# First attention: the query's norm factor moves into the exponential's scale, and epsilon into a column of the sum of squares

## What is computed

```python
q = jnp.einsum('btd,ndh->btnh', x, q_kernel)       # 16 heads of 128
kv = jnp.einsum('bsd,ckdh->cbskh', x, kv_kernel)   # 8 key/value heads
q = rms_norm(q, q_norm_scale)                      # x * rsqrt(mean(x^2) + 1e-6) * scale
k = rms_norm(k, k_norm_scale)
q = apply_rope(q, positions); k = apply_rope(k, positions)
mask = (j <= i) & (i - j < 128)
logits = jnp.einsum('btkgh,bskh->bkgts', qg * ATTN_SCALE, k)   # 2 query heads to a key head
probs = jax.nn.softmax(jnp.where(mask, logits, min), axis=-1)
enc = jnp.einsum('bkgts,bskh->btkgh', probs, v)
return jnp.einsum('btnh,nhd->btd', enc, out_kernel)
```

## Time and profile before

| | before |
|---|---|
| median of 3 runs | 1593.5 us |
| profiled execution | 1587.25 us, span of its instructions 1585.4 us |
| PE busy | 1478.0 us (93%) |
| DVE busy | 1085.6 us (68%) |
| ACT busy | 882.6 us (56%) |
| POOL busy | 403.2 us (25%) |
| first attention | 0 to about 658 us of the span |

### The profile page before, as it was taken

One profiled execution on the slowest core, in us unless ns is written; L12 is line 12 of the kernel. 1 busy time (PEld: TensorE's weight loads), 2 busy tenths in 40 slices (PEclk: granted clock), 3 DMA queues, 4 the chain that ended last, 5 costly groups with the idle time before them and its releaser, 6 DMA issues.

```text
span 1585.4 us, 24036 instructions
## 1 busy us (share of the span) xinstructions
PE 1478.0 (93%) x7582; PEld 1095.0 (69%) x7582; DVE 1085.6 (68%) x2404; ACT 882.6 (56%) x2052; POOL 403.2 (25%) x473
## 2 busy tenths in 40 slices
PE   4899999999998999799999999999879999999898
PEld 3788788878887888667777777777644444444476
DVE  6898699859976998377555455455438676767654
ACT  4777677757785777444332332332236565756556
POOL 4666566566655665200000000000000000000000
PEclk9999999999999999899999999999969899999999
DMA  6000000000000000233000000000030000000001
GB/s 236 1 1 1 1 1 1 1 3 1 1 1 3 1 1 1 66 91 90 20 1 1 0 0 0 0 0 0 2 135 1 1 1 0 0 0 0 1 14 40
DMA packets 15767, 28.54 MB, mean 18 GB/s; under 512 B 2000, under 2 KB 10064, under 8 KB 15024
## 3 DMA queue, kind: packets, MB, share of 16 engines
q1 hardware_dynamic: 15264, 26.51, 4.9%
q0 software_dynamic: 400, 0.78, 0.3%
HBM read 25.96 MB, written 2.10 MB: 18 GB/s over the span
## 4 chain that ended last, share of the span: by engine, by line
PE 73%; DVE 10%; issue 6%; POOL 5%; ACT 4%; DMA 1%; DVEq 0%; SPq 0%; ACTq 0%; POOLq 0%
PE ps L1126 13%; PE ps L1128 13%; PE ps L1127 13%; PE ps L1396 5%; PE ps L1179 5%; PE ps L1455 4%; PE ps L1225 4%; PE ps L1240 2%; PE ps L1377 2%; POOL rope L388 2%; PE ps L1523 2%; PE ps L1206 2%; DVE ssum L528 1%; PE ps L1281 1%; PE ps L1409 1%
## 5 line engine op out<-in xcount | busy, mean ns | idle before, releaser
L360 POOL TENSOR_TENSOR ln_rs<-ln_ve,minus_half 128x4 f32<-128x4 f32 x16 | 17.4, 1085 | 887.5 <-DVE ln_ve L424 887.5
L710 DVE TENSOR_REDUCE nm<-ps 128x1 f32<-128x512 f32 x256 | 168.3, 687 | 70.2 <-PE ps L1396 68.4
L1126 PE MATMUL ps<-xnT_lo,w1moe_hi 128*128 128x512 f32 x400 | 177.4, 444 | 2.4 <-DVE w2moe_lo L665 2.2
L1044 ACT ACTIVATE pT<-ps 128x512 f32<-128x512 f32 x256 | 143.5, 601 | 62.6 <-PE ps L1409 60.2
L960 ACT ACTIVATE moe_act_hi<-sg 128x512 fp32r<-128x512 f32 x100 | 63.3, 633 | 190.6 <-DVE sg L642 190.6
L1127 PE MATMUL ps<-xnT_hi,w1moe_lo 128*128 128x512 f32 x400 | 160.5, 401 | 0.0
L1128 PE MATMUL ps<-xnT_hi,w1moe_hi 128*128 128x512 f32 x400 | 159.9, 400 | 0.0
L388 POOL TENSOR_TENSOR rope<-rope 128x384 f32<-128x384 f32 x128 | 144.2, 1127 | 0.0
L632 DVE TENSOR_TENSOR sg<-ps,sg 128x512 f32<-128x512 f32 x100 | 69.1, 691 | 96.0 <-ACT sg L980 96.0
L892 ACT ACTIVATE raw<-ps 128x512 f32<-128x512 f32 x128 | 76.4, 597 | 99.3 <-PE ps L1128 97.0
L912 ACT ACTIVATE prob<-ps,nmax 128x256 f32<-128x256 f32 (+1 forms) x256 | 113.2, 457 | 30.8 <-DVE nmax L503 30.7
(11 more groups left out here) (204 smaller groups left out, 3747.3 us busy)
## 6 DMA issues: line engine op xcount, KB each, us to landing
yT<-in_w1moe SPq DMA_DIRECT2D x25, 256.0 KB, 2.6
encT<-in_wqkv SPq DMA_DIRECT2D x8, 512.0 KB, 8.7
w_in<-in_w2moe SPq DMA_DIRECT2D x25, 128.0 KB, 2.7
wo<-in_wo SPq DMA_DIRECT2D x1, 2048.0 KB, 19.1
wm<-in_wm SPq DMA_DIRECT2D x2, 1024.0 KB, 11.9
out_x<-x_res SPq DMA_DIRECT2D x4, 512.0 KB, 2.9
x_res<-in_x SPq DMA_DIRECT2D x1, 1536.0 KB, 14.7
pT<-in_c_pick SPq DMA_DIRECT2D x1, 1024.0 KB, 5.6
```

What stands on the lines that cost most here:

```text
L710: V.tensor_reduce(nm1[:, m % 2, t, col:col + 1], ps[:, 2 + i % 2, :], AX.X, ALU.max, negate=True).then_inc(s1_max, 1)
L1044: A(pT1[:, u % 2, 2 * (m % 2) + h, c, :], ps[:, 4 + e % 2, :], ACT.Exp, scale=SCALE1).then_inc(p1_ready, 1)
L1126: MM(out, left[0], right[1], start=first, stop=False)
```

## The change

1. The query heads are no longer multiplied by their factor. VectorE multiplies only the key (`kn`, 128 columns for 384), and TensorE turns the queries straight from `rope1`.
2. The query's factor is the scale operand of the exponential, one number in each row. The row maximum is then of unscaled scores, so a new VectorE instruction multiplies it by the factor: `nshift` is `nmax` times `rms`, two numbers in a row, and is the exponential's bias.
3. Epsilon is a 129th column in the buffer of the squares, set once, and is summed with them. GpSimd's addition `msq` is gone.
4. `rms` is kept in six buffers, not two, since the exponential reads it four steps later. The waits follow: GpSimd's power waits for the exponential of six steps back, ssum for the turn of the tile two before it.

```diff
-                    nc.gpsimd.tensor_tensor(msq[:, s, :], ssum[:, s, :], eps_sum[:], ALU.add).then_inc(meaned, 1)
-                    pool.wait_ge(meaned, k + 1)
-                    nc.gpsimd.tensor_tensor(rms[:, s, :], msq[:, s, :], minus_half[:, 0:3],
+                    if n >= RMS_RING:
+                        pool.wait_ge(prob_ready, k - RMS_RING + 1)
+                        pool.wait_ge(qk_normed, k - RMS_RING + 1)
+                    nc.gpsimd.tensor_tensor(rms[:, n % RMS_RING, :], ssum[:, s, :], minus_half[:, 0:3],
                                             ALU.pow).then_inc(rms_ready, 1)
                     pool.wait_ge(roped, k + 1)
-                    nc.gpsimd.tensor_tensor(rope1[:, s, :], rope1[:, s, :], rope2[:, s, :],
+                    nc.gpsimd.tensor_tensor(rope1[:, s, :].rearrange("p (h f) -> p h f", h=3),
+                                            rope1[:, s, :].rearrange("p (h f) -> p h f", h=3), rope2[:, s, :, 0:P],
                                             ALU.add).then_inc(rotated, 1)
...
                     dve.wait_ge(scored, k + 1)
+                    if m >= 2:
+                        dve.wait_ge(prob_ready, k - 1)
                     V.tensor_reduce(nmax[:, s, :], ps[:, 3 + s, :].rearrange("p (h f) -> p h f", h=2)[:, :, 0:w],
-                                    AX.X, ALU.max, negate=True).then_inc(max_ready, 1)
+                                    AX.X, ALU.max, negate=True).then_inc(maxed, 1)
+                    dve.wait_ge(maxed, k + 1)
+                    V.tensor_tensor(nshift[:, s, :], nmax[:, s, :], rms[:, m % RMS_RING, 0:2], ALU.mult
+                                    ).then_inc(max_ready, 1)
...
-                    V.tensor_tensor(qkn[:, s, :].rearrange("p (h f) -> p h f", h=3),
-                                    rope1[:, s, :].rearrange("p (h f) -> p h f", h=3),
-                                    rms[:, s, :].unsqueeze(2).to_broadcast((P, 3, P)), ALU.mult
+                    V.tensor_scalar(kn[:, s, :], rope1[:, s, 2 * P:3 * P], rms[:, m % RMS_RING, 2:3], None, ALU.mult
                                     ).then_inc(qk_normed, 1)
...
                     if n >= 2:
-                        dve.wait_ge(rotated, k - 1)
-                        dve.wait_ge(qk_normed, k - 1)
-                    V.reduce_sum(ssum[:, s, :], sq[:, s, :].rearrange("p (h f) -> p h f", h=3), AX.X
-                                 ).then_inc(summed, 1)
+                        dve.wait_ge(rms_ready, k - 1)
+                        dve.wait_ge(qk_turned, k - 1)
+                    V.reduce_sum(ssum[:, s, :], sq[:, s, :, :], AX.X).then_inc(summed, 1)
...
                         ins = A(prob[:, m % PROB_RING, h, 0:w], ps[:, 3 + s, h * 2 * P:h * 2 * P + w], ACT.Exp,
-                                bias=nmax[:, s, h:h + 1], accum_out=psums[:, s, h:h + 1])
+                                bias=nshift[:, s, h:h + 1], scale=rms[:, m % RMS_RING, h:h + 1], accum_out=psums[:, s, h:h + 1])
...
-                        ins = T(ps[:, 5 if m < EARLY_TURNS else 2, h * P:(h + 1) * P], qkn[:, m % 2, h * P:(h + 1) * P], ident[:])
+                        turned = rope1[:, m % 2, h * P:(h + 1) * P] if h < 2 else kn[:, m % 2, :]
+                        ins = T(ps[:, 5 if m < EARLY_TURNS else 2, h * P:(h + 1) * P], turned, ident[:])
```

More of the change, by code:

```diff
@@ L33 @@
 STEPS = GROUPS * TT
-RAW_RING, QK_RING, PROB_RING = 9, 4, 3
+RAW_RING, QK_RING, PROB_RING, RMS_RING = 9, 4, 3, 6
+SQ = P + 1
 LAST_LAG = 8
@@ L93, in build @@
         minus_half = sb("minus_half", [P, 16])
-        eps_sum = sb("eps_sum", [P, 3])
         spare = sb("spare", [P, 2])
@@ L107, in build @@
         ssum = sb("ssum", [P, 2, 3], where=part_a)
-        msq = sb("msq", [P, 2, 3], where=part_a)
-        rms = sb("rms", [P, 2, 3], where=part_a)
+        rms = sb("rms", [P, RMS_RING, 3], where=part_a)
         qkT = sb("qkT", [P, QK_RING, 3, P], where=part_a)
         nmax = sb("nmax", [P, 2, 2], where=part_a)
+        nshift = sb("nshift", [P, 2, 2], where=part_a)
         psums = sb("psums", [P, 2, 2], where=part_a)
@@ L117, in build @@
         rope1 = sb("rope1", [P, 2, 3 * P], where=part_a)
-        rope2 = sb("rope2", [P, 2, 3 * P], where=part_a)
-        qkn = sb("qkn", [P, 2, 3 * P], where=part_a)
+        rope2 = sb("rope2", [P, 2, 3, SQ], where=part_a)
+        kn = sb("kn", [P, 2, P], where=part_a)
         odd_head = [sb(f"odd_head_{part}", [P, SEQ], F32R, part_a) for part in ("hi", "lo")]
@@ L224, in build @@
         projected, raw_kept, squared = sem("projected"), sem("raw_kept"), sem("squared")
-        summed, meaned, rms_ready = sem("summed"), sem("meaned"), sem("rms_ready")
+        summed, rms_ready = sem("summed"), sem("rms_ready")
         roped, rotated, qk_normed = sem("roped"), sem("rotated"), sem("qk_normed")
@@ L228, in build @@
         scored, max_ready, prob_ready = sem("scored"), sem("max_ready"), sem("prob_ready")
+        maxed = sem("maxed")
         inv_ready, probn_ready = sem("inv_ready"), sem("probn_ready")
@@ L350, in _ @@
             nc.gpsimd.memset(minus_half[:], -0.5).then_inc(half_set, 1)
-            nc.gpsimd.memset(eps_sum[:], HD0 * RMS_EPS).then_inc(half_set, 1)
+            nc.gpsimd.memset(rope2[:, :, :, P:SQ], HD0 * RMS_EPS).then_inc(half_set, 1)
             pool.dma_start(ident_b[:], dram["c_ident"]).then_inc(masks_loaded, 16)
@@ L380, in attention_step @@
                     pool.wait_ge(summed, k + 1)
-                    if n >= 2:
-                        pool.wait_ge(qk_normed, k - 1)
-                    nc.gpsimd.tensor_tensor(msq[:, s, :], ssum[:, s, :], eps_sum[:], ALU.add).then_inc(meaned, 1)
-                    pool.wait_ge(meaned, k + 1)
-                    nc.gpsimd.tensor_tensor(rms[:, s, :], msq[:, s, :], minus_half[:, 0:3],
+                    if n >= RMS_RING:
+                        pool.wait_ge(prob_ready, k - RMS_RING + 1)
+                        pool.wait_ge(qk_normed, k - RMS_RING + 1)
+                    nc.gpsimd.tensor_tensor(rms[:, n % RMS_RING, :], ssum[:, s, :], minus_half[:, 0:3],
                                             ALU.pow).then_inc(rms_ready, 1)
                     pool.wait_ge(roped, k + 1)
-                    nc.gpsimd.tensor_tensor(rope1[:, s, :], rope1[:, s, :], rope2[:, s, :],
+                    nc.gpsimd.tensor_tensor(rope1[:, s, :].rearrange("p (h f) -> p h f", h=3),
+                                            rope1[:, s, :].rearrange("p (h f) -> p h f", h=3), rope2[:, s, :, 0:P],
                                             ALU.add).then_inc(rotated, 1)
@@ L533, in attention_step @@
                     rh = r3.rearrange("p (h f) -> p h f", h=3)
-                    o2 = rope2[:, s, :].rearrange("p (h f) -> p h f", h=3)
+                    o2 = rope2[:, s, :, 0:P]
                     V.tensor_tensor(o2[:, :, 0:H2], rh[:, :, H2:HD0], sin3[:, t, :, 0:H2], ALU.mult)
@@ L894, in attention_step @@
                         act.wait_ge(rotated, k - 1)
-                    A(sq[:, s, :], ps[:, s, 0:3 * P], ACT.Square).then_inc(squared, 1)
+                    A(sq[:, s, :, 0:P], ps[:, s, 0:3 * P].rearrange("p (h f) -> p h f", h=3), ACT.Square).then_inc(squared, 1)
                 if new and 2 <= n < STEPS + 2:
```

## The result

The changed kernel takes 1615.6 us (median of 4 runs, 1615.14 to 1616.13), the kernel before 1592.85 us beside it (4 runs, 1591.81 to 1593.52): ratio 1.015, interval 1.013 to 1.0171, so 23 us slower. The profiled execution took 1615.93 us with a span of 1614.1 us; the mean granted clock was 0.973, before 0.976.

The account below looks back on a forecast made before the run. TensorE was taken to set the pace at 3.83 us a step, with a VectorE-GpSimd loop close behind. Terms 14.4 + 4.4 - 6.0 + 4.0 = +16.8 us gave 1604 from the profiled execution, 1610 from the median; range 1586 to 1621.

Parts of the forecast that it names:

- item 4: Mid-batch loop, steps 8 to 31: VectorE becomes the pace, 15.90 against 15.30 us per four steps, costing 14.4 us.
- item 8: Batch ends: exponentials' second column and late nmax with nshift are uncovered, 1.0 us a batch, 4.0 in all, bounds 0 and 6.
- Item 1: GpSimd without msq: the add starts 1.77 us after ssum, not 2.12, gaining 0.35, held back by the sine products.
- Item 2: Add meets the prob multiplies: pair ends at 3.16 (add between, likelier) or 3.21 (add first), making prob and nmax 0.74 us later.
- Item 3: VectorE's rest of a step: nshift adds 0.2 us (bounds nothing to 0.56), kn replaces qkn for 0.3 less.
- item 5: Next batch's layer norm on VectorE: half of 2.2 us no longer hidden, 4.4 us over four batches, bounds 0 and 8.8.
- Item 6: First steps of a batch, before any prob: earlier add and shorter kn gain 1.5 us a batch, -6.0, bounds 0 and -9.0.
- item 7: Exponential's scale column: up to 0.10 us each, 0.2 a step, hidden by ScalarE's wait for TensorE; 25 us if uncovered.
- A: Second prob multiply keeps its turn or the add isn't ready; loop 3.6 us, TensorE still the pace: -5.4, 1588 us; chance 0.25.
- C: The exponentials' second column becomes the bound, not the collision: 25 us uncovered, 1612 us; chance 0.04.
- D: Multiple signal waits of kn, nshift and ssum add 0.1 us a step to the pace, 10 us: 1620 us; chance 0.10.
- B: Collision makes VectorE slip only in some steps, or half its price is made up: 1593 to 1596 us; chance 0.09.

Follow-up runs that it names:

- e2: The kernel before with only the epsilon column (msq removed), queries still multiplied, no nshift or second column: 1620.8 us, ratio 1.0156.
- e6: The changed kernel without nshift, the exponential's bias being the plain maximum: 1589.93 us, ratio to before 0.9993.
- e1: The changed kernel with epsilon added on GpSimd again (msq before the power): 1588.28 us, ratio to before 0.9973.
- e5: The changed kernel with the exponential's scale a constant again, the query's norm factor left out: 1609.82 us, ratio to before 1.0117.
- e4: The changed kernel with one more wait: GpSimd's add starts only after the prob multiplies of VectorE's next step: 1590.99 us.
- e11: The changed kernel with msq back on GpSimd and without nshift, the bias being the plain maximum: 1580.83 us, ratio to before 0.9947.

## Why the prediction was right

The mechanism was the one forecast and the time came in at 1615.6 for 1610, but items 4 and 8 were too small, and the difference between a median and a profiled execution hid part of that.

- Item 1, the start of the add. It was to come 1.77 after ssum's start and came 298.10 - 296.25 = 1.85. I had the power at 0.91, as in the earlier trace rows, from where msq had started. Alone it takes 1.23, so taking msq out advances the add by 0.27, not 0.35, and it is the power, not the sine products, that it waits for. It is still early enough to meet the multiplies, and e2 shows that on the kernel before this alone makes the loss.
- Item 2, the collision. The pair was to end 3.16 or 3.21 us after ssum's start, by which goes first, and ends 299.42 - 296.25 = 3.17. Of the two orders that I gave, it is the one in which the add goes ahead of both, not the one that I held likelier. For that order I had 3.21, and that it is so near is partly luck: the add came 0.08 late and took 0.90, not 1.03, so the two nearly cancel. The marks are there: the multiplies' mean went from 383 to 636 ns, VectorE's waits for the add from 47.6 us to 7.5, and TensorE's for prob from 17.6 us in 20 places to 28.5 in 49.
- Item 3. nshift, taken as 0.2 a step, measures 0.22 (e6). kn is 0.29 as thought.
- Item 4, the size that was off. Four steps take 16.16 us, not 15.90: 0.215 over TensorE's pace a step, not 0.15. 23 such steps are 4.9 of the 6.08 us that the second batch's steps 8 to 31 grew; the other 1.1 is what item 5 had for the layer norm of a batch, but as a remainder, not shown by itself. The full steps are 4.11 for 4.07, the two shorter ones 4.03 and 3.90 for 3.95 and 3.81. A miss of under 0.1 us in a loop of 4 is a third of the item, since only what lies beyond TensorE's 3.83 counts: over 96 steps it is 20.6 us, where the sum had 14.4.
- Item 6, the starts: -2.44 in the second batch, for -1.5, which is past the bound of 2.26. Over the four batches it is -5.8 for -6.0, but that agreement is luck, since the first batch gained 0.20 alone and the fourth 1.22. e1, with msq back, has -2.32 at the second batch's start and e2, with msq's removal alone, -1.07: the gain does not need msq's removal.
- Items 7 and 8, the exponential. The column takes 563 - 485 = 78 ns, hidden inside a batch (e5) as item 7 said. At the end of the second batch I had +1.0 and it was +2.97. e5, without the column, still has +1.03 there. Up to 1.5 of the 2.97 is the clock (last section), for which item 8 had nothing. At the end of the first batch, where the clock does not fall, it is +1.64, and +1.03 without the column: the column makes 0.61 there, the 0.6 of that item, and the rest is 1.0, where I had 0.4 for a late maximum and nshift. What makes the rest isn't shown by itself.
- Item 9 stands: among the waits of the first attention none for the six-step-old exponential or for the turn comes to 1 us in sum.
- The level. In medians the change costs 22.75 us for the 16.5 forecast (1610 less 1593.5), in the profiled executions 28.7 for 16.8: before's profile lay 5.6 us below its median, after's at its own. So the miss is 6 us by the one and 12 by the other. In the profiled executions steps 8 to 31 of the four batches grew by 22.7 us, for the 18.8 of items 4 and 5, and the three ends between batches by 8.9, for 3.0 by item 8.
- The rivals. A (the second multiply keeps its turn) is refuted by the pair of 1.37; what it would have brought is seen in e1 and e4, 1588 and 1591, where it had 1588. C has its part in the batch ends alone. D had 0.1 us more a step than item 4, and 0.065 more came; how much of that is the waits of short instructions isn't shown. B's time didn't follow from its own terms: with 4 to 9 us for items 4 and 5 the sum is +2 to +7, so 1595.5 to 1600.5, not 1593 to 1596. But B had the right thought in one point that I undervalued: a price counts only beyond the slack, and with 0.2 us a step less, as in e6, the kernel is level with the one before.

## What to carry to other kernels

Taking an instruction off one engine moves everything behind it, and what arrives earlier can meet what it used to miss: before such an edit, lay both engines' timelines over each other and look for two instructions that share a port. Then price against the slack to the pacing engine, not by the sum of busy times: the same collision cost 27 us where the loop was 0.2 us a step over the pace, 7 to 9 where it was about level with it (e6 against e11), and nothing where VectorE had time left. A wait that keeps two instructions apart can be the cheapest cure.

## What the runs showed of the hardware

**The add goes ahead of a multiply that began before it.** The timeline of the changed kernel, cut so that only the first of the two multiplies falls into it:

```profile
298.05 1.11 DVE L496 TENSOR_SCALAR prob<-prob,rsums 128x256 f32<-128x256 f32 x1
```

The multiply is recorded from 298.05, the add from 298.10, and it is the multiply that is held: its record is 1.11 us long and ends 0.16 after the add's end at 299.00. In e1 the add is recorded 0.32 after the first multiply, and there the add is held. The Trainium skill, SBUF — State Buffer, section Who interferes with whom, says that who issues first gets the ports for the whole instruction. That the other is held entirely agrees. Which one is first can't be told from recorded starts 0.05 us apart, and here the order of the records and that of the grant differ.

**The power alone is longer.** It takes 1232 ns with nothing ahead of it, 886 behind msq (887 in e1). From GpSimd's first instruction of a step to its add it was 297.36 - 295.88 = 1.48 us and is 298.10 - 296.89 = 1.21: msq's removal brings the add 0.27 us forward, where msq's own start to start was 0.64. The cause wasn't tested.

**TensorE's clock at the batch's end.** Before the first projection of the third batch TensorE stands idle 1.98 us in the kernel before, 2.49 in the changed one and 1.99 in e5 (PE's timeline of the changed kernel):

```profile
341.73 0.49 PE L1129 MATMUL ps<-wqkv_lo,xnT_hi 128*128 128x512 f32 x1 [2.49 <-issue]
```

Then the granted clock of the changed kernel falls. The windows view of 342 to 345 us, whose columns are busy time and instructions of PE, PEld, DVE, ACT and POOL, then the clock, the DMA share and GB/s:

```profile
342.00:345.00 3.00, 3.00 (x9) 2.31 (x9) 0.19 (x1) 0.74 (x2) 0.78 (x1) 0.54 0.03 8
```

0.54 is the lower level, 1.2 GHz, for nearly all of it; the same place in the kernel before and in e5 has 1.00. At that level 3 us of matmuls are 1.5 us of work at full speed, so up to 1.5 of the 2.97 us lost at this batch's end can be the clock's. At the end of the third batch it falls again, after 3.76 us of idle time: 507 to 510 us have 0.50. Whether the longer idle time made it fall wasn't tested, and one row speaks against so simple a reading: at 487.45 us TensorE in the kernel before had stood idle 2.47 us, and the clock stayed at 1.00.
